# Two fused LoRA layers on one core: a prologue whose queues are put in TensorE's order, with a warm-up

## What is computed

```
x = x + ffn0(cond0(x, lang))       # layer 0
x = x + ffn1(cond1(x, slot))       # layer 1
cond0: base = x @ W0.T; gates = softmax of the top 2 of (x @ Wr.T + 5*onehot(lang[b]))
       out  = base + 2 * sum_e gates_e * (x @ A0_e.T) @ B0_e.T
ffn0:  logits = c @ route_w.T; only the best expert e: out = logit_e * (c @ A0f_e.T) @ Bw_e.T
cond1: out = x @ W1.T + b1 + 2 * (x @ lora_As[slot[b]]) @ lora_Bs[slot[b]]
ffn1:  out = c @ W_base.T + b_base + 2 * sum over the top 2 experts of their adapters
```

## Time and profile before

| What | Value |
|---|---|
| median of three runs | 466.69 us |
| the profiled execution, its own time | 466.59 us |
| span of its trace, first to last instruction | 464.7 us |
| TensorE busy in the span | 447.0 us (96%) |
| VectorE, ScalarE, GpSimd busy | 306.9, 151.0, 72.6 us |
| chain that ended last: TensorE, VectorE | 83%, 12% |
| mean granted TensorE clock | 0.996 |

### The profile page before, as it was taken

The page is one execution under the profiler, slowest core; times in us unless marked ns, Lnnn a source line. Parts: engine busy times, 40 slices in busy tenths (PEclk is TensorE's granted clock), DMA queues, the critical chain, the costliest instruction groups (busy, mean ns, idle before and its releaser), DMA issues.

```text
span 464.7 us, 7813 instructions
## 1 busy us (share of the span) xinstructions
PE 447.0 (96%) x2758; PEld 414.9 (89%) x2758; DVE 306.9 (66%) x911; ACT 151.0 (32%) x314; POOL 72.6 (16%) x62
## 2 busy tenths in 40 slices
PE   4988799999999999999999999999999999999997
PEld 4977799999988898889999999999999999999986
DVE  3897637574758688578557648738747755864852
ACT  4685212322222463234233224224323423321310
POOL 2040000000002412402402222120240230220110
PEclk9999899999999999999999999999999999999999
DMA  8993131111001101104103201211210310300302
GB/s 253 383 413 138 45 149 45 47 46 44 20 35 45 50 23 49 46 18 143 48 6 107 69 28 63 98 46 62 98 45 17 135 57 1 109 9 1 107 2 90
DMA packets 15151, 37.08 MB, mean 80 GB/s; under 512 B 2439, under 2 KB 7305, under 8 KB 15118
## 3 DMA queue, kind: packets, MB, share of 16 engines
q1 hardware_dynamic: 15022, 36.66, 22.7%
q0 software_dynamic: 96, 0.00, 0.2%
HBM read 27.07 MB, written 9.59 MB: 79 GB/s over the span
## 4 chain that ended last, share of the span: by engine, by line
PE 83%; DVE 12%; ACT 2%; issue 2%; DMA 1%; SPq 0%; DVEq 0%; ACTq 0%
PE banks L1239 25%; PE banks L1241 25%; PE banks L1240 25%; PE banks L1246 4%; DVE G L789 2%; DVE WbTlo L789 2%; PE banks L1471 2%; PE banks L1283 1%; DVE left L789 1%; DMA ws_lo_raw<-in_W_dram 1%; DVE ws_lo L789 1%; PE banks L1380 0%; DVE x_raw L973 0%; DVE G_raw L1086 0%; DVE w0s_lo L789 0%
## 5 line engine op out<-in xcount | busy, mean ns | idle before, releaser
L1239 PE MATMUL banks<-G,left 128*128 128x460 f32 x224 | 88.0, 393 | 0.0
L1240 PE MATMUL banks<-G,left 128*128 128x460 f32 x224 | 82.9, 370 | 0.0
L1241 PE MATMUL banks<-G,left 128*128 128x460 f32 x224 | 82.9, 370 | 0.0
L1239 PE MATMUL banks<-WbThi,ws_hi 128*128 128x460 f32 (+1 forms) x216 | 74.6, 345 | 4.3 <-DVE WbTlo L789 3.8
L474 POOL TENSOR_TENSOR xTlo<-x_raw,xThi 128x512 fp32r<-128x512 f32 x28 | 37.9, 1374 | 238.5 <-ACT xThi L572 114.6
L1241 PE MATMUL banks<-WbThi,ws_lo 128*128 128x460 f32 (+1 forms) x216 | 73.4, 340 | 0.0
L1240 PE MATMUL banks<-WbTlo,ws_hi 128*128 128x460 f32 (+1 forms) x216 | 73.1, 338 | 0.0
L526 ACT ACTIVATE left<-x_raw 128x512 fp32r<-128x512 f32 x64 | 38.7, 627 | 59.9 <-DVE x_raw L946 29.3
L1239 PEld LDWEIGHTS banks<-WbThi,ws_hi 128*128 128x128 f32 x216 | 40.6, 188 | 8.8 <-DVE WbTlo L789 4.9
L1239 PEld LDWEIGHTS banks<-G,left 128*128 128x128 f32 x224 | 42.4, 189 | 4.5 <-DVE wzTlo L789 0.3
L1241 PEld LDWEIGHTS banks<-G,left 128*128 128x128 f32 x224 | 42.1, 188 | 4.7
(11 more groups left out here) (178 smaller groups left out, 938.2 us busy)
## 6 DMA issues: line engine op xcount, KB each, us to landing
x_raw<-in_xT_dram SPq DMA_DIRECT2D x16, 512.0 KB, 3.8
out_dram<-ybuf SPq DMA_DIRECT2D x14, 512.0 KB, 2.7
x_raw<-in_W_dram SPq DMA_DIRECT2D x8, 512.0 KB, 3.3
WbTlo_raw<-in_F_dram SPq DMA_DIRECT2D x4, 920.0 KB, 12.8
w0s_lo_raw<-in_W_dram SPq DMA_DIRECT2D x6, 512.0 KB, 9.4
Fbuf<-fe_hi_dram SPq DMA_DIRECT2D x16, 64.0 KB
WbTlo_raw<-in_F_dram SPq DMA_DIRECT2D x1, 960.0 KB, 6.6
out_dram<-ybuf SPq DMA_DIRECT2D x3, 230.0 KB, 2.4
```

What stands on the lines that cost most here:

```text
L1239: pe.matmul(out_, l[0], r[0], start=start, stop=False, **kw)
L1240: pe.matmul(out_, l[0], r[1], start=False, stop=False, **kw)
L1241: return pe.matmul(out_, l[1], r[0], start=False, stop=stop, **kw)
```

## The change

The diff is in six parts.

1. **DMA queue (SP).** A0, the first half of the first batch's tokens and F's part 0 are issued ahead of the wait for the slot numbers and ahead of the eight loads of Bs. W1's first tile is issued right behind Bs, and its two waits go.
2. **Bs** gets tiles of its own (bshi, bslo). Rows stay in the order in which they arrive, with the step as the innermost index, so that step k's 128 columns are read with a distance of eight elements (`t[:, k::K]`). VectorE's eight small subtractions become one.
3. **ScalarE and VectorE** get the order in which TensorE now wants its operands; the language bias moves ahead of R0's second half on VectorE, and the two GpSimd subtractions become VectorE's (`c0_rest`).
4. **TensorE** does the first tile's `small0` ahead of the adapters' fold, whose steps 0 to 7 were ahead of it.
5. **W1's first tile on chunk 0** (`m_chunk(0, 0)`) moves from behind the adapters' fold to between its steps 11 and 12; the later transposes and `add_lora0(1)` move behind `m_chunk(0, 1)` and into `m_chunk(0, 2)`.
6. **Warm-up:** ten matmuls of the identity by itself into bank 4, as soon as GpSimd has made the identity.

```diff
+            bshi, (bslo, bsraw) = sb("bshi", [P, D], F32R, first), twin("bslo", [P, D], first)
...
+        def adapters(t, k):
+            return t[:, k::K]
...
             load(b0raw[:, :], B0, b0_in)
+            load(a0_part(C0raw), A0, a0_in)
+            load(x_raw0[:, 0:D], xT[0, :, 0:D], x0_in[0])
+            load_f(0)
             sp.wait_ge(ids_in, 32)
             for b in range(NB):
...
-                load(w1raw[:, b * P:(b + 1) * P], lora_Bs[bass.ds(slot, 1), :, :].rearrange("s p c -> p (s c)"), bs_in)
-            load_f(0)
-            load(a0_part(C0raw), A0, a0_in)
-            load(x_raw0[:, 0:D], xT[0, :, 0:D], x0_in[0])
+                load(bsraw[:, b * P:(b + 1) * P], lora_Bs[bass.ds(slot, 1), :, :].rearrange("s p c -> p (s c)"), bs_in)
+            load_w1(0)
...
-            sp.wait_ge(bs_hi, 1)
-            sp.wait_ge(bs_lo, 1)
-            load_w1(0)
...
-            for g in range(2):
-                gp.wait_ge(c0_hi, g + 1)
...
-            act.wait_ge(w0_used, 2)
-            hi_half(bs_in, 16 * NB, k_first(ws_hi[1]), by_batch(w1raw), bs_hi)
...
+            hi_half(a0_in, 16, a0_part(C0hi), a0_part(C0raw), a0_hi)
             c0_half_part(0)
+            act.wait_ge(c0_done, 2)
+            x_first(0)
+            c0_half_part(1)
+            c0_part(0)
+            hi_half(bs_in, 16 * NB, bshi[:, :], bsraw[:, :], bs_hi)
+            c0_part(1)
             f_split(0)
-            c0_part(0)
-            c0_half_part(1)
-            hi_half(a0_in, 16, a0_part(C0hi), a0_part(C0raw), a0_hi)
-            c0_part(1)
-            x_first(0)
             act.wait_ge(d0w_done, 1)
             act.activation(D0hi[:, :], p0[:, 0:RC], ACT.Copy, scale=2.0).then_inc(d0w_hi, 1)
...
             f_split(1)
+            exp0(0)
+            w1_split(0)
+            keep_fe(0)
             f_split(2)
-            exp0(0)
-            keep_fe(0)
+            hgT_part(0)
             f_split(3)
-            hgT_part(0)
             x_first(1)
             f_split(4)
-            w1_split(0)
...
+            pe.wait_ge(ident_ready, 1)
+            for _ in range(10):
+                pe.matmul(pt[:, 0:P], ident[:, :], ident[:, :], start=True, stop=True, skip_group_check=True)
...
+            pe.wait_ge(a0_lo, 1)
+            pe.wait_ge(c0_lo, 2)
+            pe.wait_ge(d0w_lo, 1)
+            small0(0, first_tile(0), 1)
+            pe.wait_ge(bs_lo, 1)
+            pe.wait_ge(f_lo, 1)
+            fe_steps(0, K)
+            pe.wait_ge(f_lo, 2)
+            fe_steps(K, 12)
             pe.wait_ge(w1_lo, 1)
             pe.wait_ge(fe_lo, 1)
             m_chunk(0, 0)
+            turn_small(hg_ready, 1, pt_hg, hg[:, :], thg_done)
+            pe.wait_ge(f_lo, 3)
+            fe_steps(12, 2 * K)
+            add_lora0(0)
+            pe.wait_ge(f_lo, 4)
+            fe_steps(2 * K, 20)
+            turn_small(wh_ready, 1, pt_wh, wh[:, :], twh_done)
+            small0(1, first_tile(1), 2)
+            pe.wait_ge(f_lo, 5)
+            fe_steps(20, 3 * K)
+            pe.wait_ge(fe_lo, 2)
+            m_chunk(0, 1)
             turn_small(hg_ready, 2, pt_hg, hg[:, :], thg_done)
-            pe.wait_ge(fe_lo, 2)
-            m_chunk(0, 1, lambda: add_lora0(1))
+            pe.wait_ge(fe_lo, 3)
+            m_chunk(0, 2, lambda: add_lora0(1))
             turn_small(wh_ready, 2, pt_wh, wh[:, :], twh_done)
-            pe.wait_ge(fe_lo, 3)
-            m_chunk(0, 2)
             pe.wait_ge(bw_lo, 1)
             pe.wait_ge(whT_lo, 2)
```

More of the change, by code:

```diff
@@ L467, in _ @@
             gp.memset(ones[:, :], 1.0).then_inc(gp_step, 1)
-            for g in range(2):
-                gp.wait_ge(c0_hi, g + 1)
-                c0 = slice(4 * g, 4 * g + 4)
-                gp.tensor_tensor(C0lo[:, c0, ER + E:C0C], c0_sums[g], C0hi[:, c0, ER + E:C0C].bitcast(F32),
-                                 ALU.subtract).then_inc(c0_lo, 1)
             def sub(out_, a, b):
@@ L819, in _ @@
             lo_in(w0_hi, 3, w0s_lo[1][:, :], w0raw[1][:, :], w0s_hi[1][:, :], w0_lo)
[L820 to L827, removed]
             dve.wait_ge(lang_in, 16)
@@ L835, in _ @@
                                   ALU.is_equal, ALU.mult).then_inc(bias_step, 1)
+            r0_split(1)
+            for j in range(2, K):
+                lo_in(w0_hi, j + 2, w0s_lo[j][:, :], w0raw[j][:, :], w0s_hi[j][:, :], w0_lo)
+            lo_in(b0_hi, 1, b0lo[:, :], b0raw[:, :], b0hi[:, :], b0_lo)
             def c0_add(g):
@@ L839, in c0_add, with c0_rest @@
                 dve.tensor_tensor(c0_sums[g], banks[:, 4 * g:4 * g + 4, 0:RC], c0_sums[g], ALU.add).then_inc(c0_sum, 1)
-            c0_add(0)
+            def c0_rest(g):
+                dve.wait_ge(c0_hi, g + 1)
+                at = slice(4 * g, 4 * g + 4)
+                lo(C0lo[:, at, ER + E:C0C], c0_sums[g], C0hi[:, at, ER + E:C0C]).then_inc(c0_lo, 1)
+            lo_in(a0_hi, 1, a0_part(C0lo), a0_part(C0raw), a0_part(C0hi), a0_lo)
+            c0_add(0)
+            x_first(0)
+            c0_add(1)
+            c0_rest(0)
+            lo_in(bs_hi, 1, bslo[:, :], bsraw[:, :], bshi[:, :], bs_lo)
+            c0_rest(1)
             f_split(0)
-            c0_add(1)
-            lo_in(a0_hi, 1, a0_part(C0lo), a0_part(C0raw), a0_part(C0hi), a0_lo)
-            x_first(0)
             dve.wait_ge(d0w_hi, 1)
@@ L1039, in _ @@
             dve.wait_ge(bias_step, 3 + NB)
-            f_split(1)
-            gates0(0, 0, lambda: f_split(2))
+            gates0(0, 0, lambda: f_split(1))
+            w1_split(0)
             keep_fe(0)
+            f_split(2)
+            hgT_part(0)
             f_split(3)
-            hgT_part(0)
+            top1(0)
             x_first(1)
-            top1(0)
             f_split(4)
-            w1_split(0)
             whT_part(0, 0)
@@ L1302, in fe_steps @@
                     c0, n = CHUNKS[c]
-                    ins = three(m_psum(0, c), split_of(ws_hi[1], ws_lo[1], k),
+                    ins = three(m_psum(0, c), (adapters(bshi, k), adapters(bslo, k)),
                                 (Wb_of[c][0][:, k, :], Wb_of[c][1][:, k, :]), k == 0, k == K - 1)
@@ L1310, in first_tile @@
                 return lambda k: (rows(xT_first[0][half], k), rows(xT_first[1][half], k))
[L1312 to L1333, removed]
             def m_chunk(par, c, between=None):
@@ L1591 @@
         lora_As=lora_As.reshape(-1, K, P, R).transpose(0, 2, 1, 3).reshape(-1, P, K * R),
-        lora_Bs=lora_Bs.reshape(-1, R, K, P).transpose(0, 3, 2, 1).reshape(-1, P, K * R),
+        lora_Bs=lora_Bs.reshape(-1, R, K, P).transpose(0, 3, 1, 2).reshape(-1, P, R * K),
         F0=f0[None],
```

## The result

| What | Before | After |
|---|---|---|
| median of four runs | 467.53 us (466.21 to 468.63) | 472.47 us (471.68 to 473.23) |
| profiled execution, its own time | 466.59 us | 472.42 us |
| its span | 464.7 us | 470.6 us |
| TensorE busy | 447.0 us | 454.4 us |
| mean granted clock | 0.996 | 0.993 |

The changed kernel takes 1.0114 times as long, interval 1.0088 to 1.0139: slower by 1.1%. The forecast was 469.6 us with a range up to 472.4; the median lies 0.07 us above the range. The direction was right and the size too small: +2.9 us was forecast and +4.9 measured by the medians, +3.05 and +5.8 between the two profiled executions.

A forecast was written before the change was run, and what follows sets the result against it. TensorE was taken as the bound, counted up to `ffn0`'s first matmul: restart 0.4 + 2.75, old waits -3.8, old slow stretch -1.5, new waits 3.2, clock 2.0, sum +3.05 on 466.59, so 469.6 us, range 467.2 to 472.4.

The forecast's parts named there:

- rival A: Strided weight loads of Bs in 72 matmuls take twice as long: +2.4 us on the forecast, 472.0 us; chance 0.25.
- The new waits: In the fold after the restart: part 1 0.3, `m_chunk(0, 0)` 0.4, part 3 1.6, ahead of `ffn0` 0.9; together 3.2 us.
- The clock: After the 5.4 us idle stretch TensorE's clock falls to half for a while: 2.0 us lost, bounds 1.5 and 2.6.
- Rival B: Not slower: the clock does not fall at the restart, so only +1.05 us, 467.6 us; chance 0.10.
- The restart: TensorE waits for D0lo from 28.3 to 33.7, 5.4 us: 0.4 later, with 2.75 us of steps 0 to 7 undone.
- The start: The warm-up gains nothing, as W0's third block waits for its low half until 13.31: 0, bounds 2.6 gained, 0.2 lost.
- Rival C: The warm-up pays at the start: W0's third block is ready sooner, 2.6 us gained, 467.0 us; chance 0.04.
- Rival D: Faster: no clock fall and the warm-up pays, 465.0 us, or 461.8 without the new waits too; chance 0.05.
- Old waits (3.8): TensorE's three waits for F's low halves, in the view up to 75 us, go: -3.8 us.
- old slow stretch (1.5): The half-clock stretch from 50.2 to 53.4, behind the 2.4 us wait, goes: -1.5 us.

The follow-up runs named there:

- experiment 1: The changed kernel with Bs side by side again, in its old landing place and split in step order: 469.99 us, ratio to before 1.0044.
- experiment 3: The kernel before with a step's weight columns of Bs four elements (16 bytes) apart: 468.29 us, one run.
- experiment 4: The kernel before with a step's weight columns of Bs two elements (8 bytes) apart: 467.89 us, one run.
- experiment 6: The changed kernel with 20 matmuls of the identity in the idle stretch ahead of the first tile's small product: 470.74 us, ratio to before 1.0081.
- experiment 5: The changed kernel with D0hi and D0lo ahead of F's part 0 on ScalarE and VectorE: 470.21 us, ratio to before 1.0066.
- experiment 2: The kernel before with Bs kept in arrival order in its old tiles, read eight elements (32 bytes) apart: 468.19 us, ratio to before 1.0024.
- 9: The repaired version (8) with Bs again read at a distance of eight elements, in the change's own tile: 465.86 us, ratio to before 0.9971.
- 8: The changed kernel repaired: Bs side by side, sums, tokens and D0 before Bs and F's part 0, bias, part 3 and transposes moved: 461.36 us, ratio to before 0.9863.
- experiment 7: The changed kernel without the ten warm-up matmuls: 472.45 us, ratio to before 1.0113.

## Why the prediction was wrong in size

**The step that failed: the price of the strided loads.** The prediction took rival A's "a halved read may be just enough" for the likelier case and put 0 into the sum for 72 matmuls. They cost 4.9 us of TensorE time (24 x 0.125 and 48 x 0.039), and 2.8 us net in the trace of experiment 1, where other waits come back without them. The prediction's own sign of being wrong, steps 0 to 7 more than 0.12 us apart at the full clock, came true: 0.240. With 4.9 for 0, the waits at 1.56, the clock at 1.5 and the restart 0.34 later, the forecast's +3.05 becomes the +6.15 of the account above; +5.95 was measured. Rival A (472.0) came true, and it was itself too small: it doubled the load from 0.115 to 0.23 but charged only the 240-column steps. By its own numbers a load of 0.23 is also above what 460 columns need at 272 in 0.13 (0.22; they stood 0.207 apart), so those had to pay too; I didn't compare the two. That 472.0 still lies so near the measured 472.47 is luck: the 1.9 us that it left out and the 2.1 by which the waits and the clock were counted too high nearly cancel. With no row against rival A, 0.25 was too small a chance for it. The Trainium skill's rule that the prediction set beside A spoke for it, and experiments 3 and 4 agree with it.

**The new waits (3.2)** were too many: 1.56. Part 3 cost 0.8 instead of 1.6, and the waits for part 1 (0.3) and `m_chunk(0, 0)` (0.4) did not occur. With fast loads (experiment 1) the waits were 2.6 us, so about 1.0 of the difference goes with the slow loads, behind which VectorE has more time; the other 0.6 was counted too high. The last, ahead of `ffn0`, was 0.8 as against 0.9.

**The clock (2.0, bounds 1.5 and 2.6)** was 1.5, the lower bound; 1.56 and 1.7 us by experiment 6. Rival B, no fall, did not occur: all four runs after the change have a mean grant of 0.993, as one stretch of 6.4 us at half gives (3.2 of 470.6 us).

**The restart (33.7, idle 5.4)** held: 34.04 and 5.39. The restart came 0.34 later than forecast, about as much as B0's fold ended later (0.37). The chain was the one written down, with the tokens' low half at 1.23 us, as taken, not 2.36 (from the timelines of DVE and ACT):

```profile
27.14 1.23 DVE L779 SCALAR_TENSOR_TENSOR w0s_lo<-x_raw,w0s_hi 128x1024 fp32r<-128x1024 f32 x1 [1.71 <-ACT w0s_hi L517]
...
31.42 2.16 DVE L779 SCALAR_TENSOR_TENSOR WbTlo<-WbTlo_raw,WbThi 128x1920 fp32r<-128x1920 f32 x1
33.49 0.29 DVE L779 SCALAR_TENSOR_TENSOR D0lo<-banks,D0hi 128x136 fp32r<-128x136 f32 x1
```

```profile
31.29 0.27 ACT L555 ACTIVATE D0hi<-banks 128x136 fp32r<-128x136 f32 x1
```

**The start (0)** held: W0's third block at 13.70 with a wait for w0s_lo ahead of it. That is 0.4 later than before, more than the bound of 0.2 lost, but experiment 5, with the same start, has it at 13.31. There are 0.02 us between the times with and without warm-up. Rivals C and D fall with it.

**Old waits (3.8) and old slow stretch (1.5)** went as said. The path and the order of the waits were right; the term that no row could price, and that stood at 0, decided.

**A slip in its sums:** on 466.59, 1.05 + 1.5 less 0.2 and 1.05 + 2.6 with 1.1 give 468.9 to 471.3, not 468.7 to 471.0. The range of 467.2 to 472.4 does not hang on it.

## What to carry to other kernels

Before a weight is read at a distance, compare the load's new time with the distance of every matmul that uses it, the wide ones too: what is hidden behind 272 columns may not be hidden behind 240, and at twice the time not behind 460. Keep the columns side by side, or 8 bytes apart at most (16 and 32 were slow here), or rearrange them while splitting. And an operation's price depends on where the waits are: the same strided loads cost about 1, 2.5 and 4.5 us in three orders of this program (experiments 2, 1 and 9).

## What the hardware showed that I had not expected

- **A distance of two is nearly free, one of four is not.** Weight loads of 128 columns took 189 ns side by side, 194 at 8 bytes (in a group with W1's), 287 at 16 and 291 at 32 (same groups), 341 at 32 bytes alone.
- **The clock falls after short rests, but not each time.** After 1.34 us it fell in the profile of 8 and not in that of 9. The kernel before shows it as well. Its 41 runs beside the experiments have a mean granted clock of 0.996 in 21 (465.7 to 467.34 us) and of 0.993 in 20 (467.54 to 471.49): a second fall. Experiment 4, which keeps the order of before, has two falls in its trace, the known one at about 51 to 55 and one that shows where the second can lie, behind the 1.9 us wait for D0lo:

```profile
34.80:38.00 3.20, 3.20 (x15) 3.20 (x15) 0.18 (x2) 0.00 (x0) 0.00 (x0) 0.51 1.03 400
```

  The profile on which I predicted was of the first kind, and its 2.06 us of rest had seemed harmless. The four runs before the change are, by their times, two of either kind (466.21 and 466.69, 468.38 and 468.63), which is why the medians differ by 4.9 us and the traces by 5.9. What decides between the two kinds was not found.
- **A warm-up that works can be worth nothing.** It brought 2.4 GHz 2.7 us forward between two traces (from 9.51, experiment 7, to 6.84; the kernel before, also without it, got there at 12.5), and the medians differ by 0.02 us, since the operand that TensorE wants at 13 us is made by two other engines.
